# GpSimd's program written out as straight code, with the indices of its row transfers read in place (a four-layer GNN block, one core)

## What is computed

```python
h = relu(layernorm(x)); x = x + L0(h)   # degree-normalised sum over edges, @ W.T + b, relu, + h
h = relu(layernorm(x)); x = x + L1(h)   # per edge relu(h[src] @ W[type] + b), summed by dst
h = relu(layernorm(x)); x = x + L2(h)   # two graph convolutions (128 -> 128 -> 64), two dense layers
h = relu(layernorm(x)); x = x + L3(h)   # attention: per-edge score, softmax over dst, sum of z[src]
```

## Time and profile before

| | |
|---|---|
| median of 3 runs | 7405.13 us (7396.46 to 7417.42) |
| the profiled execution, its own time | 7414.55 us |
| its span in the trace | 7413.1 us |
| POOL busy | 5014.6 us, 68% |
| DVE busy | 5058.8 us, 68% |
| PE busy | 3484.1 us, 47% |
| ACT busy | 2902.2 us, 39% |

### The profile page before, as it was taken

How to read it: one execution, slowest core, us unless ns; L and a number is a source line. 1 busy time by engine, 2 the same in 40 slices (tenths; PEclk the granted TensorE clock), 3 DMA queues, 4 the chain that set the end, 5 groups by cost and what they waited for, 6 DMA issues and landing times. The chain is left out here.

```text
span 7413.1 us, 112938 instructions
## 1 busy us (share of the span) xinstructions
PE 3484.1 (47%) x18429; PEld 2609.0 (35%) x18429; DVE 5058.8 (68%) x20258; ACT 2902.2 (39%) x7124; POOL 5014.6 (68%) x4720
## 2 busy tenths in 40 slices
PE   7655256656668888830006777100886233333000
PEld 1111155555666666620005555000664122222000
DVE  7999488776778888877767777222774355555554
ACT  0366111118863333345546666000331255554222
POOL 0377578884457777766657773676778677776677
PEclk9766599998989999965558888555998555555555
DMA  7488578879973333346669999222996333333443
GB/s 291 156 287 288 164 131 142 140 121 312 337 223 91 91 91 91 93 128 175 176 189 366 368 362 320 54 52 58 335 346 213 89 104 103 104 103 91 125 136 114
DMA packets 1168531, 1326.62 MB, mean 179 GB/s; under 512 B 231276, under 2 KB 968790, under 8 KB 1157939
## 3 DMA queue, kind: packets, MB, share of 16 engines
q1 hardware_dynamic: 961680, 1002.76, 42.1%
q0 software_dynamic: 206768, 323.00, 18.7%
HBM read 706.30 MB, written 646.54 MB: 182 GB/s over the span
## 5 line engine op out<-in xcount | busy, mean ns | idle before, releaser
L724 POOL DMA_INDIRECT dense<-t_xs,ends x784 | 787.4, 1004 | 356.3 <-issue 183.1
L1841 PE MATMUL ps<-dense,w 128*128 128x256 f32 x3136 | 730.2, 386 | 189.1 <-DVE dense L1552 156.7
L564 POOL DMA_INDIRECT t_src<-tot,sidx x392 | 624.6, 1593 | 188.1 <-issue 91.8
L1841 PEld LDWEIGHTS ps<-dense,w 128*128 128x128 f32 x3136 | 581.4, 190 | 306.1 <-DVE dense L1552 195.5
L1765 PE MATMUL ps<-oneh_c,oneh_p 128*128 128x395 f16 x1568 | 457.7, 429 | 278.4 <-DVE oneh_c L901 269.3
L796 ACT ACTIVATE estd<-emv,epsc 128x2 f32<-128x2 f32 (+1 forms) x588 | 174.0, 296 | 1034.1 <-DVE emv L779 1034.1
L699 POOL DMA_INDIRECT t_yacc<-dense,gq x392 | 455.8, 1163 | 135.6 <-issue 110.3
L1552 DVE SCALAR_TENSOR_TENSOR dense<-xT 128x256 f32<-128x256 f32 x1568 | 544.0, 420 | 2.7 <-ACT xT L2024 2.5
L724 POOL DMA_INDIRECT dense<-t_y,ends x392 | 372.8, 951 | 241.3 <-DVE ends L1645 150.8
L662 POOL DMA_INDIRECT out_rows<-dense,sidx x392 | 390.1, 995 | 183.3 <-issue 110.4
L662 POOL DMA_INDIRECT t_xs<-dense,sidx x392 | 399.3, 1019 | 123.7 <-issue 65.2
(11 more groups left out here) (327 smaller groups left out, 11987.1 us busy)
## 6 DMA issues: line engine op xcount, KB each, us to landing
dense<-t_xs SPq DMA_DIRECT2D x78, 1320.0 KB, 8.8
dense<-in_x SPq DMA_DIRECT2D x156, 640.0 KB, 5.6
t_xs<-dense SPq DMA_DIRECT2D x98, 528.0 KB
t_xs<-hb SPq DMA_DIRECT2D x78, 660.0 KB
t_src<-dense SPq DMA_DIRECT2D x99, 512.0 KB, 6.3
t_sum<-dense SPq DMA_DIRECT2D x98, 512.0 KB
t_src<-dense SPq DMA_DIRECT2D x78, 640.0 KB
dense<-t_src SPq DMA_DIRECT2D x78, 640.0 KB
```

What stands on the lines that cost most here:

```text
L564: gp.indirect_dma_start(t_src, bass.IndirectOffsetOnAxis(ap=sidx[:, p.k, c:c + 1], axis=0), tot[:, p.k, c, :], None, compute_op=ALU.add).t ...
L724: gp.indirect_dma_start(rows[:, p.k, c, :], None, table, bass.IndirectOffsetOnAxis(ap=gidx[:, p.k, c:c + 1], axis=0)) \
L1841: i = nc.tensor.matmul(ps[:, o:o + 2 * P], w1[:, k, :], xm[:, p.w, k, :], start=(k == 0), stop=(k == R - 1))
```

## The change

- A new helper `pairs` writes out all 196 steps of a GpSimd loop by pair, and `group_loop` is gone: the 49 groups are written out as well. GpSimd's program has no hardware loop left except in the first convolution.
- Every indexed transfer reads its index from a kept table: `src_i`, `dst_i`, `keyg`, and two that are filled on VectorE, `half_i` (`src * 2 + 1`, in the space of `typ_i`) and `keyi` (`keyend * 2` for E1, `keyend` for the last phase). The copies into `gidx`, `didx`, `sidx` (of E1 and the last phase) and `gq` go, with the waits for them.
- In place of the ring, `gath` waits until the slot of its rows was read (`E1["tx"]`, `E2["sc"]`, `R3["second"]`, six pairs earlier).
- The lags change: in E1 VectorE's go from 3, 4, 6, 8 to 0, 1, 3, 5, and GpSimd's `ends1` from 8 to 5; in E2 VectorE's go from 3, 4, 5 to 0, 1, 2; in E3 from 5 to 0.
- In `gather_ahead` the register load for the next group stands after the fourth gather of a group, and the store of the group before after the seventh. In `late_pool` the next group's load is issued ahead of a group's writes, and the wait for the landing of the group before stands after its fifth write instead of its second.

```diff
+def pairs(*stages):
+
+    for q in range(NPAIR + max(lag for _, lag in stages)):
+        for fn, lag in stages:
+            if 0 <= q - lag < NPAIR:
+                fn(Pair((q - lag) // UNROLL, (q - lag) % UNROLL))
...
+        half_i = typ_i
...
+            stored_blocks = blocks_of(0)
+            for g0 in range(NGROUP):
+                if g0 >= SLOTS:
+                    gp.wait_ge(P0["scat"][g0 % SLOTS].sem, P0["scat"][g0 % SLOTS].after(g0 // SLOTS * 16))
                     gp.sem_inc(tick, 1)
-                gp.tensor_copy(gq[:, u, :], keyg[:, bass.ds(g0 * GROUP, GROUP)]).then_inc(P0["index"].sem, 1)
-                stored_blocks = gp.value_load(blocks[0:1, bass.ds(g0, 1)], min_val=1, max_val=NB + 1)
                 gp.wait_ge(P0["written2"].sem, P0["written2"].after(stored_blocks))
                 gp.sem_inc(tick, 1)
-                gp.wait_ge(P0["index"].sem, P0["index"].after(g0 + 1))
-                gp.sem_inc(tick, 1)
...
+                gather(g0, 0, 4)
+                if g0 + 1 < NGROUP:
+                    stored_blocks = blocks_of(g0 + 1)
+                gather(g0, 4, 7)
+                if g0:
+                    store(g0 - 1)
+                gather(g0, 7, GROUP)
+            store(NGROUP - 1)
...
             def ends(p):
                 gp.wait_ge(ready.sem, ready.after(p.q + 1))
                 gp.sem_inc(tick, 1)
                 for c in range(2):
-                    gp.indirect_dma_start(target, bass.IndirectOffsetOnAxis(ap=sidx[:, p.k, c:c + 1], axis=0),
+                    gp.indirect_dma_start(target, bass.IndirectOffsetOnAxis(ap=index[:, p.q * 2 + c:p.q * 2 + c + 1], axis=0),
...
-            group_loop(gp, (load, 0), (begin, 1), (landed, 2), (go_on, 1))
+            load(0)
+            for n in range(NGROUP):
+                if n + 1 < NGROUP:
+                    load(n + 1)
+                gp.wait_ge(s["load"][n % SLOTS].sem, s["load"][n % SLOTS].after(n // SLOTS * 16 + 16))
+                gp.sem_inc(tick, 1)
+                write(n, 0, 5)
+                if n:
+                    landed(n - 1)
+                write(n, 5, GROUP)
+            landed(NGROUP - 1)
...
             def gath(p):
-                gp.wait_ge(s["ring"].sem, s["ring"].after(p.q + 1))
-                gp.sem_inc(tick, 1)
+                if needed(p.n):
+                    gp.wait_ge(read.sem, read.after(p.q - RING + 1))
+                    gp.sem_inc(tick, 1)
                 for c in range(2):
                     gp.indirect_dma_start(rows[:, p.k, c, :], None, table,
-                                          bass.IndirectOffsetOnAxis(ap=gidx[:, p.k, c:c + 1], axis=0)) \
+                                          bass.IndirectOffsetOnAxis(ap=index[:, p.q * 2 + c:p.q * 2 + c + 1], axis=0)) \
...
-            if per:
-                nc.vector.tensor_scalar(sidx[:, p.k, :], keyend[:, bass.ds(p.q * 2, 2)], float(per), None, ALU.mult)
...
-            gath1 = rows_pool(gp, E1, t_half[0:2 * N, :], gn)
-            ends1, close1 = run_pool(gp, R1, R1["second"], t_half, tot1, Z1, last1, 2)
-            pair_loop(gp, (gath1, 0), (ends1, 8))
+            gath1 = rows_pool(gp, E1, t_half[0:2 * N, :], half_i, gn, E1["tx"])
+            ends1, close1 = run_pool(gp, R1, R1["second"], t_half, keyi, tot1, Z1, last1, 2)
+            pairs((gath1, 0), (ends1, 5))
...
+            nc.vector.tensor_scalar(half_i[:, 0:T], src_i[:, 0:T], 2.0, 1.0, ALU.mult, ALU.add)
+            nc.vector.tensor_scalar(keyi[:, :], keyend[:, :], 2.0, None, ALU.mult)
...
-            pair_loop(v, (e1_stats, 3), (e1_scales, 4), (mask, 6), (e1_sums, 8), (e1_ring, 0))
+            pair_loop(v, (e1_stats, 0), (e1_scales, 1), (mask, 3), (e1_sums, 5))
...
-            pair_loop(v, (e2_ring, 0), (e2_stats, 3), (e2_scales, 4), (e2_sums, 5))
+            pair_loop(v, (e2_stats, 0), (e2_scales, 1), (e2_sums, 2))
...
-            pair_loop(v, (e3_ring, 0), (e3_sums, 5))
+            pair_loop(v, (e3_sums, 0))
```

More of the change, by code:

```diff
@@ L166, in wide_loop @@
         at(b)
[L169 to L186, removed]
 class Pair:
@@ L433, in gnn @@
         keyg = sb("keyg", [P, NGROUP * GROUP], I32)
-        gq = sb("gq", [P, SLOTS, GROUP], I32)
         nexti = sb("nexti", [P, 2], I32)
@@ L486, in gnn @@
         A0 = phase("node", NB + 1, LN + "nb h", {"ld": slots(16), "sto": slots(16)})
-        P0 = phase("late", 1, f"index:{NGROUP} written2:{NB + 1}",
+        P0 = phase("late", 1, f"written2:{NB + 1}",
                    {"load": [16 * GROUP * len(range(u, NGROUP, SLOTS)) for u in range(SLOTS)],
@@ L499, in gnn @@
         X0 = phase("rows", NB + 1, "", {"load": [16 * len(range(u, NB + 1, WIDE)) for u in range(WIDE)]})
-        E1 = phase("edge", NPAIR, "ring bn mv std rs nb h tx txc masked xw relu back", GP)
+        E1 = phase("edge", NPAIR, "bn mv std rs nb h tx txc masked xw relu back", GP)
         R1 = phase("runs", NPAIR, "first second", SC)
@@ L503, in gnn @@
         Z1 = phase("last_runs", 1, "made close total last:16")
-        E2 = phase("edge", NPAIR, "ring joined bn mv std rs sc nb h", GP)
+        E2 = phase("edge", NPAIR, "joined bn mv std rs sc nb h", GP)
         R2 = phase("runs", NPAIR, "first second scaled", SW)
@@ L525, in gather_ahead, with blocks_of, gather @@
         def gather_ahead(gp):
[L527 to L530, removed]
+            def blocks_of(g0):
+                return gp.value_load(blocks[0:1, g0:g0 + 1], min_val=1, max_val=NB + 1)
+            def gather(g0, lo, hi):
+                u = g0 % SLOTS
+                for c in range(lo, hi):
+                    gp.indirect_dma_start(gs2[u][:, c, :], None, t_src[0:N, :],
+                                          bass.IndirectOffsetOnAxis(ap=keyg[:, g0 * GROUP + c:g0 * GROUP + c + 1], axis=0)) \
+                        .then_inc(P0["load"][u].sem, 16)
@@ L565, in body @@
                                           tot[:, p.k, c, :], None, compute_op=ALU.add).then_inc(R0["scat"][p.k].sem, 16)
-            pair_loop(gp, (body, 0))
+            pairs((body, 0))
             for k in range(RING):
@@ L654, in sums_tensor, with run_pool @@
             pair_loop(pe, (body, 0))
-        def run_pool(gp, s, ready, target, rows, z, total, per=1):
+        def run_pool(gp, s, ready, target, index, rows, z, total, per=1):
             def ends(p):
@@ L676, in late_pool @@
         def late_pool(gp, s, written, runs, target, rows):
[L678 to L697, removed]
+            def load(n):
+                g0 = NGROUP - 1 - n
+                gp.dma_start(rows[n % SLOTS].rearrange("p c f -> p (c f)"),
+                             runs[g0 * GE:(g0 + 1) * GE, :].rearrange("(p c) f -> p (c f)", c=GROUP)) \
+                    .then_inc(s["load"][n % SLOTS].sem, 16)
@@ L733, in run_start, with run_sums @@
             v.wait_ge(z["made"].sem, z["made"].after(1))
-        def run_sums(v, s, p, totals, in0, in1, per=1, free="scat"):
+        def run_sums(v, s, p, totals, in0, in1, free="scat", each=32):
             width = in0.shape[-1]
@@ L1200, in _ @@
             end_phase(gp, PO)
-            gath3 = rows_pool(gp, E3, t_y, gy)
-            pair_loop(gp, (gath3, 0))
+            gath3 = rows_pool(gp, E3, t_y, src_i, gy, R3["second"])
+            pairs((gath3, 0))
             carry_pool(gp, R3, Z3, t_run3, msg[:, 0, 0, 0:H2])
@@ L1208, in edge_rows @@
             def edge_rows(p):
-                gp.wait_ge(A3["ring"].sem, A3["ring"].after(triple(p) + 1))
-                gp.sem_inc(tick, 1)
                 if needed(p.n):
@@ L1557, in e1_sums @@
                 v.wait_ge(E1["back"].sem, E1["back"].after(p.q + 1))
-                run_sums(v, R1, p, tot1, *[ps[:, BACK[p.w] + c * P:BACK[p.w] + (c + 1) * P] for c in range(2)], 2)
+                run_sums(v, R1, p, tot1, *[ps[:, BACK[p.w] + c * P:BACK[p.w] + (c + 1) * P] for c in range(2)])
             nc.vector.memset(tot1[:, :, :, D:XW1], 0.0)
@@ L1685, in _ @@
             end_phase(v, VE)
-            def score_ring(p):
-                lo = p.u % RING * 2
-                nc.vector.tensor_scalar(ends[:, :, lo:lo + 6], ends_i[:, :, bass.ds(p.q * 2, 6)], 1.0, None, ALU.mult) \
-                    .then_inc(A3["ring"].sem, 1)
-            score_ring(Pair(0, 0))
             def meanwhile(p):
@@ L1696, in meanwhile @@
                     score(p.plus(-4))
-                if p.u % 3 == 0 and not (isinstance(p.q, int) and p.q + 3 >= NPAIR):
-                    score_ring(p.plus(3))
             def scores(p):
```

73 lines of the change are left out of this document (28 added, 45 removed).

## The result

The changed kernel takes **8594.55 us** (median of 4 runs, 8594.29 to 8602.26); the kernel before, measured beside it, 7407.62 us (4 runs). The ratio is 1.1595, 95% interval 1.1578 to 1.1613: slower by 16%. The forecast was 8515 us, range 8430 to 8670.

What follows compares the result with a forecast made beforehand. GpSimd's starting of transfers was taken to bound E1, E3, scores and last phase, VectorE E2. 7414.55 + 1204 - 20 - 50 - 15 - 8 = 8525, less 9 to the median, gave 8515 us, range 8430 to 8670.

Steps and rivals of the forecast that it cites:

- E1: Phase bounded by GpSimd, 1076 us before; the new order of lags was to add 1204 us, bounds -38 and +76.
- E2: VectorE's phase, 611 us before: dropping the ring copy and its wait was to gain 50 us, bounds 20 and 60.
- the circle: In E1, a pair's writes wait for VectorE's step, which waits for the newest gather, queued behind earlier writes; 87 in 100.
- VectorE's step: In E1, VectorE's work from the start of the statistics to the end of the second sum: 4.42 us without the copy.
- The turn: In E1, one time round the circle: 11.7 us where 5.4 stood, bounds 11.5 and 12.1, for 190 turns.
- The transfers: In E1, GpSimd's two writes with the gap between them, 2.26 us, and two gathers with theirs, 2.20 us.
- the way back: In E1, from the end of VectorE's second sum to the start of GpSimd's write: 0.88 us.
- The late gather: Copy and wait go in 49 groups, 34 us, less 0.3 us each for the register load: -20 us, bounds -34 and -10.
- The decoder: Waits for a landing within a group go, 19 us, copies count nothing: -15 us in all, bounds 0 and -35.
- The feared stretch: In the decoder, part of the saved wait may come back as longer transfers, whose mean was 1163 ns.
- that the circle does not close: Rival for E1: GpSimd runs on at its own 5.4 us and only the gains are left, 7312 us; 4 in 100.
- That straight code is not fed in time: Rival on GpSimd's longer written-out code: 1.5 us more at some 50 places, +75 us, 8590 us in all; 8 in 100.

Runs made afterwards that it cites:

- lags 6, 7, 8: The changed kernel with GpSimd's writes of totals in E1 at lag 6, 7 or 8 instead of 5: 7516.5, 7303.0 and 7291.7 us.

## Why the prediction was right

- **The mechanism** was the one named, and five runs show it. Distance opens the circle (lags 6, 7, 8), the lag alone closes it in the kernel before, and time added to VectorE's step comes through whole (2.68 us a turn of 2.69). The idle time stands before the writes, is ended by L740, and comes 195 times.
- **The turn** was mis-sized: 11.7 us forecast, 12.17 measured between the second sums of pair 0 and of pair 190, which over 190 turns is 89 of the 94 us by which E1 was missed; 4 more are in the last five pairs. By terms: VectorE's step 4.69 in the mean (4.65 in most turns) for 4.42, since I took a step from the end of the phase, which is written out, for one in the loop (the run with VectorE's E1 written out confirms this term: its turn is 11.90 us, and E1 was 53 us shorter). The transfers, 2.30 and 2.26 for 2.26 and 2.20, and the way back, 0.92 for 0.88, make 0.14. The stalls of 1.5 us over a normal gap, every 23 turns, make 0.07; the rows of before show one gap of that size (the 1.8 of the earlier trace rows, in the encoder, right behind a wait), and I took it for crowding. Whether it is the same stall is not shown. The landing was right, 1.65 for 1.64.
- **The total** was 80 us over the forecast and within the range, but E1 by itself was not within its bounds: +1298 against at most +1280 (1204 + 76). That the whole came nearer is in part luck, since the late gather, E2 and the decoder gained 41 us more than forecast.
- **The late gather** gained 36 us, not 20: the 0.3 us a group charged to the register load was wrong, and its true value was the lower end, nothing. The page "DMA: Bandwidth & Descriptors" of the Trainium skill gives about 600 ns for the load; here none of it is exposed at either place, with a transfer of 0.95 us being started in front of it. The measurement decides: no cost.
- **E2** -58 for -50, within its bounds, with VectorE still the bound, at 2.65 us a pair where 2.7 were to be left. **The decoder** -32 for -15, in three parts by the timelines. Between the writes of one group 20 us of idle time went, the 19 that were counted. The feared stretch gave 5 us back (mean 1175 ns for 1163). And between two groups, where the index copy stood, 57.6 us became 41.9. This is the term that was put at nothing, because the copies looked half hidden by the gaps; but a copy that takes 0.23 us in most groups took more than 0.5 in 13 of the 49, and up to 1.56 (the kernel before):

```profile
5330.26 1.56 POOL L685 COPY gq<-keyg 128x8 int32 x1
```

- **Scores** +14 for 0: missed, and open.
- **The rivals**: that the circle does not close was wrong. That straight code is not fed in time was tested by itself and is nothing (1.0002); the stalls that look like it are also there in the loop. The Trainium skill's page "Runtime: NRT & Kernel Launch" says in its section on instruction fetch that code is fetched ahead in sequence; the 1.0002 agrees with that.

## What to carry to other kernels

When two engines feed each other through in-order lists, count the distance round the whole circle: from a transfer to its use on the second engine, and from that use to what stands in front of the next transfer on the first. Lags that are all shortened by the same number look unchanged, yet here the three steps taken away closed the circle, and the 126 us gained in the late gather, E2 and the decoder (36, 58 and 32) went under in the 1298 lost in E1. The ring of copies itself did not hold the two lists apart: with the ring kept and lag 5 the loss is there (ratio 1.178), and without it and with lag 8 it is not (0.983). So when a ring is removed, remove it as work and keep the distance that was set beside it (here one number), and the removal pays. Two steps more opened the circle in the middle of the phase, and the third was still worth some 5 us at its ends.

## What the runs showed of the hardware that was not expected

- In E1 of the four kernels whose circle is closed, GpSimd shows a gap of 1.8 to 2.1 us without a releaser every 92 indexed transfers, in loop code and in straight code, by number and not by time. Each stands right behind a write that had been waited for; at lags 7 and 8, where GpSimd does not wait, none is seen in the middle of E1. In the scores a smaller one, 0.56 to 0.95 us, comes every 96 transfers, in every kernel. What they are, no run here tells.
- VectorE's step with two waits on its own semaphores is 0.23 us shorter written out than in its hardware loop (4.42 and 4.65 us), though the same change on GpSimd gives nothing (ratio 1.0002). Why the two differ was not tested.
- GpSimd takes 0.81 to 0.92 us from the end of the instruction waited for to its next start, where it has a gap of 0.30 when nothing is waited for (0.81 in the earlier trace rows, 0.88 in the earlier trace rows, 0.92 above).
